# A Mamba and mixture-of-experts kernel: the chunk state product from rounded halves, and at other places of the matmul order

## The reference

```
state_local = einsum('bcjGH,bcjGH,bcjGn,bcjGHp->bcGHnp', decay_to_end, dt, B, x)
state_at_end = d_r * s_l + s_r                      (scanned over the chunks)
y_inter = einsum('bciGH,bciGn,bcGHnp->bciGHp', decay_from_start, C, state_at_start)
y = y_intra + y_inter
```

## Time and profile before

| | |
|---|---|
| median of 3 runs | 2308.38 us (2302.44 to 2312.76) |
| the profiled execution | 2305.35 us |
| its span, first to last instruction | 2303.6 us |
| mean granted TensorE clock | 0.995 of full speed |
| TensorE busy (matmul) | 2252.9 us, 98% |
| VectorE busy | 1363.3 us, 59% |
| ScalarE busy | 882.4 us, 38% |
| GpSimd busy | 693.7 us, 30% |

### The profile page before, as it was taken

One profiled execution on the slowest core, in us unless ns is written; L12 is line 12 of the kernel. 1 busy time (PEld: TensorE's weight loads), 2 busy tenths in 40 slices (PEclk: granted clock), 3 DMA queues, 4 the chain that ended last, 5 costly groups with the idle time before them and its releaser, 6 DMA issues.

```text
span 2303.6 us, 41271 instructions
## 1 busy us (share of the span) xinstructions
PE 2252.9 (98%) x16412; PEld 2003.2 (87%) x16412; DVE 1363.3 (59%) x3201; ACT 882.4 (38%) x1563; POOL 693.7 (30%) x534
## 2 busy tenths in 40 slices
PE   6999999999998999999999999999999999999998
PEld 6999998777798899999998999998999999777787
DVE  6777762222228677777777777778777763223322
ACT  5232321233327555554555555455323231223321
POOL 1244443112220433233332223331144444122222
PEclk9999999999999999999999999999999999999999
DMA  8776525989844111111111111104376532988949
GB/s 273 263 260 209 164 84 181 306 282 284 236 89 138 45 30 36 28 28 29 28 28 29 28 28 29 28 22 169 125 282 224 199 104 78 312 291 286 290 83 183
DMA packets 129279, 334.73 MB, mean 145 GB/s; under 512 B 24450, under 2 KB 45186, under 8 KB 118400
## 3 DMA queue, kind: packets, MB, share of 16 engines
q1 hardware_dynamic: 80592, 236.63, 28.7%
q0 software_dynamic: 48496, 95.46, 18.1%
HBM read 218.25 MB, written 172.77 MB: 170 GB/s over the span
## 4 chain that ended last, share of the span: by engine, by line
PE 87%; DVE 4%; ACT 4%; DMA 3%; issue 1%; SPq 0%; DVEq 0%; POOL 0%; ACTq 0%; POOLq 0%
PE m_p_ab L1687 3%; PE m_p_x L1687 3%; PE m_p_x L1689 3%; PE m_p_x L1688 3%; PE m_p_ab L1689 3%; PE m_p_ab L1688 3%; PE p_up_b L769 3%; PE p_x_b L873 3%; PE p_x_a L873 3%; PE p_up_a L769 3%; PE p_gate_b L769 2%; PE m_p_y L1808 2%; PE m_p_y L1809 2%; PE p_up_b L771 2%; PE p_up_b L770 2%; PE p_gate_b L770 2%
## 5 line engine op out<-in xcount | busy, mean ns | idle before, releaser
L2004 DVE SCALAR_TENSOR_TENSOR m_xt<-m_ssm,m_convw,m_xt 128x256 f32<-128x256 f32 x384 | 211.9, 565 | 55.2 <-ACT m_ssm L1553 46.0
L1687 PE MATMUL m_p_ab<-m_ht_hi,m_wi_b_hi 128*128 128x256 f32 x576 | 164.5, 286 | 3.8 <-ACT m_ssm L1553 3.4
L506 POOL DMA_INDIRECT slot_rows<-a_hr,a_slot_now x128 | 128.4, 1003 | 131.3 <-PE p_gate_a L771 81.0
L506 POOL DMA_INDIRECT slot_rows<-b_hr,b_slot_now x128 | 128.9, 1007 | 129.5 <-PE p_gate_b L771 80.1
L1688 PE MATMUL m_p_ab<-m_ht_lo,m_wi_b_hi 128*128 128x256 f32 x576 | 161.3, 280 | 0.0
L1689 PE MATMUL m_p_ab<-m_ht_hi,m_wi_b_lo 128*128 128x256 f32 x576 | 161.2, 280 | 0.0
L769 PE MATMUL p_gate_a<-a_hts_hi,a_w_hi 128*128 128x256 f32 x512 | 148.4, 290 | 1.8 <-DVE a_hts_lo L1068 1.8
L1457 POOL TENSOR_TENSOR m_state_dec<-m_state,m_etot 128x1024 f32<-128x1024 f32 x31 | 74.0, 2386 | 248.7 <-ACT m_etot L1569 248.7
L769 PE MATMUL p_gate_b<-b_hts_hi,b_w_hi 128*128 128x256 f32 x512 | 147.0, 287 | 0.3 <-DVE b_hts_lo L1068 0.3
L769 PE MATMUL p_up_a<-a_hts_hi,a_w_hi 128*128 128x256 f32 x512 | 145.5, 284 | 0.0
L769 PE MATMUL p_up_b<-b_hts_hi,b_w_hi 128*128 128x256 f32 x512 | 145.4, 284 | 0.0
(11 more groups left out here) (378 smaller groups left out, 7346.7 us busy)
## 6 DMA issues: line engine op xcount, KB each, us to landing
a_ew<-in_ew SPq DMA_DIRECT2D x32, 1536.0 KB, 7.2
b_ew<-in_ew SPq DMA_DIRECT2D x32, 1536.0 KB, 7.3
after_ffn<-a_zeros POOLq DMA_DIRECT2D x6, 2048.0 KB, 9.2
out<-b_zeros POOLq DMA_DIRECT2D x6, 2048.0 KB, 10.1
slot_rows<-a_zeros POOLq DMA_DIRECT2D x1, 8336.0 KB, 37.1
a_rows<-slot_rows SPq DMA_DIRECT2D x32, 260.5 KB, 8.4
b_rows<-slot_rows SPq DMA_DIRECT2D x32, 260.5 KB, 8.2
m_x<-after_ffn SPq DMA_DIRECT2D x16, 512.0 KB, 3.6
```

The lines of the kernel that those rows point to most:

```text
L506: g_.indirect_dma_start(out=xg, out_offset=bass.IndirectOffsetOnAxis(ap=slot_now[r % HR][:, at:at + 1], axis=0), in_=hr[r % HR][:, j, :], ...
L1687: t.matmul(out, l_hi, r_hi_, start=first, stop=False)
L2004: ins_ = v.scalar_tensor_tensor(xt[:, m, :], ssm[:, m, i:i + BM], convw[:, m, i:i + 1], xt[:, m, :], ALU.mult, ALU.add)
```

## The change

The state product becomes three rounded products of halves: B (`btok_hi`, `btok_lo`) by xs (`xs_hi`, `xs_lo`). ScalarE makes btok_hi and xs_hi (`b_hi`, `state_in_hi`), VectorE btok_lo and xs_lo (`b_lo`, `state_in_lo`). Memory is shared: xs_hi and btok_lo lie where cdec and decay of tile 0 lay, so xs_hi of tile 0 waits for the first four heads of the y product (`y_half`) and btok_lo for all of it; xs_lo is written over xs; btok_hi lies where cb lay. The order changes as follows.

- TensorE: state product 0 moves into the C projection, between its third and its fourth group of three matmuls (in the last step behind the second layer's transposes); state product 1 moves behind `out_product(n, 0)`.
- VectorE: xs_lo and btok_lo come ahead of `skip_part(n, 0)`; `norm_rest(n+1)` moves behind `gated(n, 0)`; xs_lo of tile 1 takes the place of `add_state(n, 1)`, which moves into the next step, behind `add_out(n, 0)`.
- ScalarE: btok_hi and xs_hi of tile 0 come ahead of `head(n+1)`, xs_hi of tile 1 ahead of `tokens_out(n+1)`.
- GpSimd's order and waits are as before.

```diff
         cum_rows = sb("cum_rows", [P, BM], F32R)
+        btok_hi = Region(nc, "m", sb.next)("btok_hi", [P, TM, P], F32R)
         cb = sb("cb", [P, TM, P])
...
         x[2], x[1] = sb("x2", [P, TM, D]), sb("x1", [P, TM, D])
-        cdec_both = sb("cdec", [P, TM, NH, P])
-        decay_both = sb("decay", [P, TM, NH, P])
+        rounded = Region(nc, "m", sb.next)("rounded", [P, 2, TM, NH, P], F32R)
+        weights = sb("weights", [P, 2, TM, NH, P])
+        cdec_both, decay_both = weights[:, 0, :, :, :], weights[:, 1, :, :, :]
         cdec, decay = [cdec_both[:, j, :, :] for j in range(TM)], [decay_both[:, j, :, :] for j in range(TM)]
+        xs_hi, btok_lo = rounded[:, :, 0, 0:NH // 2, :], rounded[:, 1, 0, NH - TM:NH, :]
         xdt_both = sb("xdt", [P, TM, NH, HP])
         xdt = [xdt_both[:, j, :, :] for j in range(TM)]
+        xs_at = sb.next
         xs, state = sb("xs", [P, NH, HP]), sb("state", [P, NH, HP])
+        xs_lo = Region(nc, "m", xs_at)("xs_lo", [P, NH, HP], F32R)
+        by_half = lambda part: part[:].rearrange("p (b h) q -> p b h q", b=2)
         la_wide = sb("la", [P, (TM - 1) * NH + P])
...
         nabs_ready, soft_ready, la_ready = sem("nabs_ready"), sem("soft_ready"), sem("la_ready")
-        soft_exp, dtt_set = sem("soft_exp"), sem("dtt_set")
+        y_half, state_hi, state_lo = sem("y_half"), sem("state_hi"), sem("state_lo")
         pick_ready, cum_t_ready, cum_hi_ready, cum_lo_ready = (
...
             def head(n):
...
                 if is_(n, 0):
-                    act.wait_ge(dtt_set, 1)
+                    act.wait_ge(pick_ready, 1)
                 copy_job(n, J_DT, dtt[0:CR, :], CR)
...
             def tokens_out(n):
-                wait(act, s_full, n * TM)
+                if n > 0:
+                    act.wait_ge(state_lo, n * 3 - 1)
                 copy_job(n, J_TOK, tok[:, :])
+
+            def b_hi(n):
+                act.wait_ge(ab_free, n * JOBS + J_TOK + 1)
+                act.wait_ge(decay_ready, n * TM + TM)
+                a.activation(btok_hi[:], btok, ACT.Copy).then_inc(state_hi, 1)
+
+            def state_in_hi(n, j):
+                act.wait_ge(xs_ready, n * TM + j + 1)
+                if j == 0:
+                    act.wait_ge(y_half, n + 1)
+                else:
+                    act.wait_ge(s_full, n * TM + j)
+                a.activation(xs_hi, by_half(xs), ACT.Copy).then_inc(state_hi, 1)
...
             def softplus(n):
                 act.wait_ge(nabs_ready, n + 1)
-                a.activation(nabs[:], nabs[:], ACT.Exp).then_inc(soft_exp, 1)
-                act.wait_ge(soft_exp, n + 1)
+                a.activation(nabs[:], nabs[:], ACT.Exp).then_inc(soft_ready, 1)
+                act.wait_ge(soft_ready, 2 * n + 1)
                 a.activation(nabs[:], nabs[:], ACT.Ln, bias=c.ones[:, 0:1]).then_inc(soft_ready, 1)
...
             def block_(n):
...
                     turned(n + 1)
+                    b_hi(n)
+                    state_in_hi(n, 0)
                     head(n + 1)
                 else:
+                    b_hi(n)
+                    state_in_hi(n, 0)
                     phase.follow.act.early(1)
...
                     if more:
+                        state_in_hi(n, 1)
                         tokens_out(n + 1)
...
                     ones2 = c.ones[:, :].unsqueeze(1).to_broadcast([P, TM, P])
-                    a.activation(dtt[:].rearrange("p (j t) -> p j t", j=TM), ones2, ACT.Copy, scale=0.0).then_inc(dtt_set, 1)
+                    a.activation(dtt[:].rearrange("p (j t) -> p j t", j=TM), ones2, ACT.Copy, scale=0.0)
                     a.activation(cum_rows[:].rearrange("p (j t) -> p j t", j=TM), ones2, ACT.Copy, scale=0.0)
...
-            def project(n, job, col):
+            def project(n, job, col, between=None):
                 if is_(n, 0):
...
                                ht_hi[:, k, :], ht_lo[:, k, :], k == 0, k == KD - 1)
+                    if between and k == KD - 2:
+                        between()
                 mm.then_inc(ab_full, 1)
...
             def to_tokens(n):
...
                     mm = t.matmul(out, state[:, hd, :], cdec[j][:, hd, :], start=False, stop=True)
+                    if j == 0 and hd == NH // 2 - 1:
+                        mm.then_inc(y_half, 1)
                 mm.then_inc(y_full, 1)
...
             def state_product(n, j):
-                pe.wait_ge(xs_ready, n * TM + j + 1)
+                pe.wait_ge(state_lo, n * 3 + 2 + j)
                 if is_(n, NM - 1) and j == 0:
...
                 for b in range(2):
-                    mm = t.matmul(p_cr[:, b, :], btok[:, j, :],
-                                  xs[:, :, :].rearrange("p h q -> p (h q)")[:, b * 512:(b + 1) * 512],
-                                  start=True, stop=True)
+                    hi, lo = (part.rearrange("p h q -> p (h q)") for part in (
+                        xs_hi[:, b, :, :], xs_lo[:, b * NH // 2:(b + 1) * NH // 2, :]))
+                    mm = three(p_cr[:, b, :], btok_hi[:, j, :], btok_lo[:, j, :], hi, lo, True, True)
                 mm.then_inc(s_full, 1)
...
             def out_product(n, j):
...
-            def head(n):
+            def head(n, between=None):
                 pe.wait_ge(ht_ready, n * 2 + 2)
                 project_dt(n)
-                project(n, J_C, C0)
+                project(n, J_C, C0, between)
                 project(n, J_B, B0)
...
             def block_(n):
...
                 y_product(n, 0)
-                state_product(n, 0)
                 if not is_(n, NM - 1):
-                    head(n + 1)
+                    head(n + 1, lambda: state_product(n, 0))
                     y_product(n, 1)
-                    state_product(n, 1)
                     to_tokens(n + 1)
...
                     phase.follow.pe.early(0)
+                    state_product(n, 0)
                     y_product(n, 1)
...
                 out_product(n, 0)
+                if not is_(n, NM - 1):
+                    state_product(n, 1)
...
             def early(u):
...
             def decay_steps(n):
-                dve.wait_ge(soft_ready, n + 1)
+                dve.wait_ge(soft_ready, 2 * n + 2)
                 dve.wait_ge(cr_full, n * TM)
...
                                 ALU.subtract).then_inc(y_ready, 1)
+
+            def b_lo(n):
+                dve.wait_ge(state_hi, n * 3 + 1)
+                dve.wait_ge(y_full, n * TM + 1)
+                v.tensor_tensor(btok_lo, btok, btok_hi[:].bitcast(F32), ALU.subtract).then_inc(state_lo, 1)
+
+            def state_in_lo(n, j):
+                dve.wait_ge(state_hi, n * 3 + 2 + j)
+                v.tensor_tensor(by_half(xs_lo), by_half(xs), xs_hi.bitcast(F32), ALU.subtract).then_inc(state_lo, 1)
...
             def add_state(n, j):
...
                         add_out(n - 1, 0)
+                        add_state(n - 1, 1)
                     convolve(n, 0)
...
                     times_dt(n, 1)
-                    if more:
-                        norm_rest(n + 1)
+                    state_in_lo(n, 0)
+                    b_lo(n)
                     skip_part(n, 0)
...
                         gated(n, 0)
+                        norm_rest(n + 1)
                     else:
...
                         time_steps(n + 1)
-                        add_state(n, 1)
+                        state_in_lo(n, 1)
                     halves(n, 1)
...
                         decay_steps(n + 1)

```

## The result

The changed kernel takes 2314.8 us (median of 22 runs, 2307.5 to 2321.2), the kernel before 2304.6 us in its 22 runs: **ratio 1.0037, with 95% between 1.0027 and 1.0047**. By the ratio it is slower by 8.5 us, and so are the two profiled executions (2313.96 less 2305.35, 8.6); the two medians lie 10.2 apart. Each is inside the 0.5% that the prediction called no difference, and more than this many runs leave uncertain. The forecast, +11.7, is 3 us too high by the ratio and 1.5 by the medians. The profiled execution took 2313.96 us where 2317.1 was forecast. The forecast median, 2320.1, is 5.3 too high: 3.8 of that comes from the median of three runs, 2308.38, that it was put on, against 2304.6 in 22.

A forecast was written before the change was run, and what follows sets the result against it. TensorE, busy for 98% of the span, was taken as the bound; +0.71 us in each of 15 steps (+10.7) and +1.0 in the last gave +11.7, on the 2308.38 median 2320.1 us, range 2297 to 2326.

The forecast's parts named there:

- The mechanism: GpSimd and VectorE exclude each other at a shared SBUF port, delaying halves(0) and opening a 1.4 us TensorE gap.
- the serial sum: decay_inputs(1), gated, decay_state(1), norm_rest one after another until 1101.51, then halves(0); output product late, step 0.71 us longer.
- Rival 1: No lasting collision of GpSimd and VectorE: halves(0) ends before 1101.5, 9.5 us faster, 2298.9; chance 0.18.
- rival 2: Only two-input VectorE operations are held, so norm_rest runs beside decay_state(1): 2 us faster, 2306; chance 0.15.
- The first test: State product 0 and y product 1: add_state allows y product 1 at 1097.48, TensorE arrives 1097.50; nothing lost, no margin.
- my two bounds: State product's cost for changing bank or breaking into C's accumulation: nothing, or 0.09 us a product, 2.8 in all.
- The sum: Whole kernel: +10.7 us over 15 steps and +1.0 in the last, +11.7 in all.
- The last step: Mamba's last step: the rounding lengthens the state chain before y product 1, costing +1.0 us (0 to 1.3).
- The clock rival: The new TensorE gap brings the clock down, 1.5 us more in each of 15 steps: 2343 us; chance 0.08.
- the mechanism that I held likeliest: The forecast's own case, port collision before the output product: +7 to +17 us, 2315 to 2325; chance 0.52.

The follow-up runs named there:

- experiment 3: Changed kernel with GpSimd's decay_state(1) held back until halves(n, 0) is done: 2295.7 us, ratio 0.9956 to the kernel before.
- experiment 1: Changed kernel with norm_rest back at its old place, ahead of the rounding: 2298.6 us, ratio 0.9979 to the kernel before.
- experiment 7: Changed kernel with plain state products at the new places, no rounding, norm_rest at its old place, last step as before: 2311.0 us, ratio 1.0022 to the kernel before.
- Experiment 5: Changed kernel with one more 128x1024 GpSimd product just before decay_state(1): 2351.9 us, ratio 1.0185 to the kernel before.
- experiment 6: Changed kernel with the rounded state products at their old places in TensorE's order, norm_rest still behind gated: 2337.8 us, ratio 1.0124 to the kernel before.
- experiment 8: Changed kernel with ScalarE's xs_hi copy waiting for all of y product 0 instead of half: 2336.0 us, ratio 1.0107 to the kernel before.

## Why the prediction was right, and where it was off

**The mechanism** held, link by link. `gated`, `decay_state(1)` and `norm_rest` were each held as the serial sum said, with each time in the table above met within 0.02 us up to `halves(0)`. Rival 1 (no lasting collision) and rival 2 (only two-input operations are held) are refuted by `norm_rest` at 2.57 in place of 0.99, and by experiment 3, which restores 0.99 by moving only GpSimd's product. That a one-input `norm_rest` is held was the step with the least in the trace of before behind it; the Trainium skill (SBUF — State Buffer, "SBUF: two separate sides") says it of VectorE in a two-port mode, and the 2.57 here agrees. That `norm_rest` runs in such a mode is read from its pace, 0.45 for 512 elements, and no row names the mode.

**The first test** came out as worked: y product 1 at the forecast time within 0.01, with no gap. That there was no margin is seen in experiment 1, where `norm_rest` put ahead of the rounding made a step 0.34 longer than in experiment 3, with y product 1 starting 0.26 after `add_state` ended.

**The term that was mis-sized** is the step from the end of `halves(0)` to the first output matmul, "1101.54 to 1102.77, first output matmul 1103.03". I took 0.26 for it, from `add_state` to a waiting plain y matmul. The output product starts 0.06 after `halves` ended (1052.72 less 1052.66), in all fifteen steps alike; its second matmul follows 0.34 on. That makes the gap 1.16, not 1.4, and the step 0.57 longer in the aligned pair, not 0.71. That is 0.15 a step, 2.2 us over 15. I had taken the delay of one product for another's. It is not that one is rounded and the other plain: the plain transposes of `x_to_tokens` start 0.05 after ScalarE in one place, in the changed kernel

```profile
762.53 1.06 ACT L1611 ACTIVATE m_xt<-m_xt 128x1024 f32<-128x1024 f32 x1 [3.25 <-DVE m_xt L2034]
...
763.64 1.09 PE L1820 MATMUL m_p_x<-ident,m_xt 128*128 128x128 f32 x8 [2.06 <-ACT m_xt L1611]
```

and 0.15 after VectorE in another. Why a waiting y product needs 0.26 stays open. The rounded products measured 1.38 and 1.40 for the 1.37 taken, so changing the bank, and for product 0 standing inside C's accumulation, costs 0.01 to 0.03 together, near the lower of my two bounds.

**The sum**, on the two profiled executions: the first `decay_inputs(0)` comes 1.4 late (766.42 against 765.04), ahead of any changed step; in the other profiles of these kernels this lies between 764.0 and 767.7, so it is scatter. The fifteen steps take 815.35 against 808.04: +7.3, where I had +10.7; 2.2 of the difference is the term above, and 1.2 is the scatter of steps, 53.80 to 54.07 before and 54.29 to 54.59 after, by which the pair that I aligned (+0.57) is not the mean (+0.49). The longest steps, two before and one after, are those of the slower pace of experiment 7. The last step costs +1.07 to y product 1, where I had +1.0:

```profile
1581.78 2.72 POOL L1470 TENSOR_TENSOR m_xs<-m_xdt,m_to_end 128x1024 f32<-128x1024 f32 x1 [0.89 <-DVE m_xdt L2050]
...
1590.63 0.46 PE L1835 MATMUL m_p_y<-m_weights,m_xdt 128*128 128x128 f32 x2 [1.75 <-DVE m_state L2088]
```

8.85 from one to the other, before 7.78. From there to the end the changed kernel takes 1.14 less: the kernel before had some 3.4 us at half clock just behind the Mamba stage, and the changed one had not. The kernel before:

```profile
1590.00:1640.00 50.00, 48.03 (x322) 43.50 (x321) 38.74 (x67) 24.68 (x30) 1.01 (x1) 0.97 0.36 126
1605.00:1607.00 2.00, 2.00 (x10) 1.90 (x10) 2.00 (x3) 0.18 (x1) 0.00 (x0) 0.50 0.40 154
```

And the changed kernel:

```profile
1590.00:1640.00 50.00, 47.15 (x328) 43.22 (x329) 41.12 (x69) 24.56 (x29) 1.01 (x1) 1.00 0.40 141
```

1.38, 7.31, 1.07, less 1.14: the 8.6 by which the spans differ. Of these 7.31 and 1.07, 8.4 together, are the change's own, to be set against the 11.7 forecast; the other two are scatter of this pair of executions and happen to cancel.

**The clock rival** did not come about: 1.00 over the 13 steps with a gap of 1.16 in each. Experiment 5 brought it in with a gap of 2.74, in twelve steps of fifteen, and at 1.6 us a step, near the 1.5 that the rival had priced; in the other three the same gap left the clock alone. Between these, experiment 6 has waits of 1.53 and 0.97 in each step and experiment 8 one of 2.17 in its last step, and the granted clock is 1.00 over 800 to 1500 us in the one and over 1600 to 1630 us in the other.

**Where I could have seen more.** The chances put 0.60 on no measurable difference or faster, and the mechanism that I held likeliest sat on the line; with that term as measured it is 9.5 us, inside. The 0.05 of a waiting rounded product stood in the trace of before: one projection of each step waits for ScalarE's `m_ssm` and starts its weight load 0.05 after that ends (1128.62 less 1128.57 in the step behind the one shown). What the prediction did not say is that the loss hung on one place in VectorE's list: moving `norm_rest`, or delaying `decay_state(1)`, is worth 13 to 19 us, which its own times already contained.

## What to carry to other kernels

When a change starts an elementwise product on GpSimd earlier, list every VectorE operation with its sources in SBUF that will then run beside it, and lay them out one after the other instead of side by side: a product of 1.9 us cost TensorE 1.2 us here in each of 15 steps. A GpSimd product with slack should be held until VectorE's critical operation has passed; that one wait was worth 19 us here, more than the 10.9 that the rounded products were to save. And an operation moved behind another in VectorE's order must be judged with the width that it will have there (2.57), not with that of its old place (0.99).

## What the runs showed of the hardware

- Between GpSimd and VectorE the port goes to the engine that waits as soon as the other's instruction ends, one instruction each. So a chain of short VectorE operations paid once for each GpSimd instruction: two of 0.54 took 2.57 together beside one product and 4.15 (2.11 each) beside two. I had taken the order for `decay_state(1)`, but not seen that it is strict.
- A VectorE operation that had waited ended 1.07 to 1.08 after GpSimd's end at 1024 elements, whether it began 0.4 us before that end (the kernel before), 0.6 (experiment 1) or 0.8 (the changed kernel). Operations with one input in PSUM kept their time beside GpSimd: `add_state` 1.22 beside `decay_inputs(1)`, and `skip_part` 2.15 beside `decay_state(1)` in experiment 3.
- From VectorE's end to a waiting matmul it took 0.05 to 0.06 for the rounded output and state products, 0.15 for the plain transposes, and 0.26 for the plain y product, in all profiles alike.
- Matmuls of 256 columns ran at one of two paces, 0.113 to 0.114 or 0.118 from start to start, for most of a step's 120 at a time, at full granted clock: 0.24 us a step. No run shows what chooses.
- Rounded 128x512 matmuls ran at the same 0.23 each in the state product as in the output product, though they changed the bank midway and stood inside another product's accumulation.
